# Shared keys and values of the third attention computed during the second feed-forward

## Chip, cores and metric

One core of a Trainium2 chip runs the program. The metric is the device time of one execution in microseconds; of several executions the median is told. 
## What is computed

Eight layers in a row work on x, 32 sequences of 128 tokens with 128 features, with a context of the same shape. Each layer normalises x, computes something, scales it by a gate and adds it to x. The order is attention, feed-forward, four times over:

```python
x = x + tanh(g_xattn[0]) * L0_xattn(layernorm(x), ctx, ctx, ...)   # 16 heads
x = x + tanh(g_ffn[0])   * L0_ffn(layernorm(x), w1, w2)            # quantised
x = x + tanh(g_xattn[1]) * L1_xattn(layernorm(x), ctx, ctx, mask)  # one head
x = x + tanh(g_ffn[1])   * L1_ffn(layernorm(x), gate, up, down)    # quantised, gated
x = x + tanh(g_xattn[2]) * L2_xattn(layernorm(x), ctx, ctx, ...)   # 16 heads, one key and value head
x = x + tanh(g_ffn[2])   * L2_ffn(layernorm(x), switch_w, ...)     # 8 experts
x = x + tanh(g_xattn[3]) * L3_xattn(layernorm(x), ctx, mask, ...)  # 16 heads
x = x + tanh(g_ffn[3])   * L3_ffn(layernorm(x), W_exp, ...)        # butterfly
```

The change concerns L2_xattn. Its 16 query heads share one key head and one value head of 8 features; keys and values depend on the context alone, and the context is an input:

```python
qh = (q @ w_q).reshape(B, L, 16, 8).transpose(0, 2, 1, 3)
kvp = c @ w_kv                      # c is the context, w_kv is 128 x 16
k, v = (kvp[..., :8], kvp[..., 8:])
attn_prob = softmax(einsum('bhid,bjd->bhij', qh, k) / sqrt(8))
out = einsum('bhij,bjd->bhid', attn_prob, v)
```

## The kernel before

The program is written per engine. Each engine has its own list of instructions in a fixed order, and semaphores tie them together. x, the context and its transpose contextT (a column per token) stay in SBUF the whole time, one tile of 128x128 per sequence, 32 tiles.

**Second feed-forward (bit_ffn, called for "F1").** It works on pairs of tiles, 16 of them (NP). A step j touches several pairs at different ages. VectorE takes the largest values of the normalised rows of pair j+4 (L1890), adds the result of pair j to x (L1895), multiplies gate and up part of pair j+2 (L1902), takes their largest values (L1910), works out scales (L1917 to L1929) and rounds pair j+2 (L1942). GpSimd rounds the rows of pair j+4 (L806) and signals bit_qx. TensorE multiplies pair j+3 with the gate and up weights (L1454, L1455), pair j+1 with the down weights (L1467), waits for bit_qx, transposes pair j+4 into bank 6 (L1475) and then the hidden values of pair j+2 (L1485). ScalarE applies silu to pair j+3 (L1043), normalises pair j+5 (L1055), copies the transposed rows (L1062) and the transposed hidden values (L1068) out of PSUM. The first iterations of the third attention are placed between the last steps (TENSOR_BETWEEN, SCALAR_BETWEEN).

**Attention (attention, called for "L0", "L2" and "L3").** Its iteration t does one tile. Each iteration has two halves; a half computes scores for half of the heads of tile t, keys by queries (L1268), and for tile t+2, queries by keys (L1271). VectorE takes row maxima from the latter (L1728), splits them into three bf16 parts, and L1282 subtracts them from the scores as a small matmul; ScalarE takes the exponentials (L944), TensorE multiplies them with the values (L1300). Queries, keys and values are made for four tiles at once, a quad (NQ is 8, QT is 4). In "L2" and "L3" the quad c is transposed at t = 4c - 6 (L1366), the queries are made in the same iteration (L1417), the keys at 4c - 5 with one matmul over 512 columns of contextT (L1373) and the values at 4c - 3 with four matmuls of 128x128 (L1422). All three use one PSUM bank (quad_bank, bank 5) in turn. For "L2" the weights l2_wkv hold the 8 columns of w_kv sixteen times, so keys and values come out once per head. ScalarE copies queries to q_all (L968), keys to k_all (L974) and values into vals (L982), and makes four masked copies of the keys, k_one (L954), on which the queries-by-keys scores run. q_all, k_all, k_one and vals have two halves, for an even and an odd quad.

From t = 7 on the iterations of "L2" also route tiles to the experts: a normed tile is transposed and multiplied with switch_w (L1341, L1405), VectorE picks the expert (hot_experts, L1859 to L1865, after iterations 10, 14, ...), and GpSimd scatters rows to HBM (L856). Where the order of work around the change is set: by the order in which these functions issue, and by semaphores such as t_kn (keys copied), t_ve (values copied), bit_qx (rows rounded).

The context itself (not transposed) is last read by the second attention (L1519). Its memory takes the experts' weights once the scores of the third attention are done (L541, L564).

## Time and profile before

| | us |
|---|---|
| median of 3 runs (1108.57 to 1113.24) | 1110.26 |
| the profiled execution | 1101.8 |
| its span in the profile | 1100.0 |
| TensorE busy, of the span | 918.0 (83%) |
| VectorE busy | 740.9 (67%) |
| ScalarE busy | 684.4 (62%) |
| GpSimd busy | 469.5 (43%) |

In fortieths of the span (27.5 us each) it reads 0.5 to 0.9 from about 250 to 440 us, and 0.9 nearly everywhere else, where 0.9 stands for 90% or more. The stage views further down give these figures for chosen stretches. Busy time says which engine has little room; which engine ends a wait is read from the timeline.

### The profile page before, as it was taken

The numbers are of one execution on the slowest core, as the hardware profiler recorded it, in microseconds if no ns is written. First come the engines' busy times: TensorE is split into PE (matmuls) and PEld (weight loads), VectorE is DVE, ScalarE is ACT, GpSimd is POOL, SyncE is SP. The second block draws the span as 40 slices with busy tenths as digits, with TensorE's granted clock in tenths as the row PEclk, the third lists the DMA queues.
The fourth block names the chain that finished last, engine by engine and source line by source line (L and its number), as shares of the span: only waits on it lengthen the run. The fifth ranks groups of instructions, "written<-read, shape, count | busy, mean of one in ns | idle before, by whom it ended". The sixth has DMA issues, their size and how long they took to land.

```text
span 1100.0 us, 29173 instructions
## 1 busy us (share of the span) xinstructions
PE 918.0 (83%) x9573; PEld 572.6 (52%) x9573; DVE 740.9 (67%) x2005; ACT 684.4 (62%) x1499; POOL 469.5 (43%) x999
## 2 busy tenths in 40 slices
PE   3898889885658665699999988888689899999898
PEld 2744444443436433434545444778664445544698
DVE  2567877756978799868888874246336767666344
ACT  3556666646856566767777643545466677775466
POOL 5422367751134424201143444668541249885200
PEclk9999999995668768899999996989899999999999
DMA  6978778627699993000000002666621001110011
GB/s 177 159 94 93 67 82 90 97 28 183 127 163 167 164 163 41 1 1 2 2 11 11 11 17 60 175 174 181 204 89 49 2 3 41 40 41 2 8 34 36
DMA packets 300443, 84.95 MB, mean 77 GB/s; under 512 B 211929, under 2 KB 287097, under 8 KB 300314
## 3 DMA queue, kind: packets, MB, share of 16 engines
q1 hardware_dynamic: 293962, 67.11, 37.9%
q0 software_dynamic: 5488, 15.88, 4.5%
q8 instruction: 78, 1.28, 0.5%
q10 hardware_dynamic: 864, 0.27, 0.1%
q14 instruction: 51, 0.42, 0.1%
HBM read 50.70 MB, written 35.51 MB: 78 GB/s over the span
## 4 chain that ended last, share of the span: by engine, by line
PE 59%; DVE 22%; issue 9%; POOL 4%; ACT 3%; DMA 2%; SPq 1%; another core or an unknown queue 1%; DVEq 0%; ACTq 0%; POOLq 0%
PE bank L1268 15%; DVE nmax L1728 9%; PE bank L1300 6%; PE bank L1390 3%; PE bank L1580 3%; PE bank L1282 3%; PE bank L1592 3%; PE bank L1634 3%; PE bank L1626 3%; PE bank L1271 2%; DVE small L1910 2%; PE bank L1399 2%; PE bank L1258 2%; PE bank L1417 1%; DVE stats L1663 1%
## 5 line engine op out<-in xcount | busy, mean ns | idle before, releaser
L1728 DVE TENSOR_REDUCE nmax<-bank 128x8 f32<-128x1024 f32 x192 | 234.7, 1223 | 120.7 <-PE bank L1271 119.3
L944 ACT ACTIVATE probs_space<-bank 128x1024 f32<-128x1024 f32 x192 | 196.7, 1024 | 145.4 <-PE bank L1282 144.4
L1268 PE MATMUL bank<-q_one,k_all 32*128 32x512 f32 x768 | 216.7, 633 | 32.5 <-DVE nmax L1728 28.9
L1271 PE MATMUL bank<-k_one,q_all 32*128 32x512 f32 x768 | 214.2, 631 | 2.2 <-DVE nmax L1728 0.9
L1300 PEld LDWEIGHTS bank<-probs_space,vals 128*32 128x32 f32 x3072 | 73.2, 110 | 121.8 <-issue 121.4
L1300 PE MATMUL bank<-probs_space,vals 128*32 128x128 f32 x3072 | 125.6, 282 | 0.0
L1268 PEld LDWEIGHTS bank<-q_one,k_all 32*128 32x128 f32 x768 | 62.1, 185 | 61.6 <-issue 57.8
L954 ACT ACTIVATE k_one<-k_all,one_head 128x512 f32<-128x512 f32 x96 | 68.9, 722 | 20.8 <-DVE k_all L1752 19.3
L640 POOL TENSOR_TENSOR var_b<-stats 128x8 f32<-128x8 f32 (+3 forms) x33 | 7.4, 225 | 170.9 <-DVE stats L1663 168.8
L715 POOL CAST nmax_parts<-nmax 128x16 bf16<-128x16 f32 x64 | 12.7, 198 | 157.6 <-DVE nmax L1728 144.2
L1282 PE MATMUL bank<-nmax_one,ones_bf 12*128 12x512 bf16 x384 | 78.0, 379 | 0.0
L1762 DVE TENSOR_TENSOR nmax_one<-bank,max_row 128x512 bf16<-128x512 bf16 x96 | 65.4, 682 | 2.2 <-PE bank L1347 2.2
L868 POOL DMA_INDIRECT token_rows<-early,slot_row_int x46 | 49.0, 1064 | 41.8 <-DVE early L2098 34.1
L1663 DVE BATCH_NORM_STATS2 stats<-x 128x6 f32<-128x128 f32 x230 | 61.3, 288 | 5.3 <-DMA x<-in_x_dram 2.3
L1580 PE MATMUL bank<-xn,context 128*128 128x128 f32 x368 | 53.5, 292 | 13.4 <-issue 12.0
L2098 DVE TENSOR_TENSOR early<-bank,context 128x128 f32<-128x128 f32 x46 | 13.4, 291 | 72.1 <-PE bank L1592 65.2
L1271 PEld LDWEIGHTS bank<-k_one,q_all 32*128 32x128 f32 x768 | 58.6, 184 | 5.3 <-issue 4.2
L1580 PEld LDWEIGHTS bank<-xn,context 128*128 128x128 f32 x368 | 48.9, 207 | 15.5 <-issue 13.7
L699 POOL TENSOR_TENSOR late<-bf_up,late 128x512 f32<-128x512 f32 x36 | 56.8, 1598 | 0.1
L647 POOL TENSOR_TENSOR var_a<-var_b,minus_half 128x8 f32<-128x8 f32 (+3 forms) x33 | 54.0, 1638 | 2.6
L960 ACT ACTIVATE q_one<-q_all,one_head 128x512 f32<-128x512 f32 x80 | 54.6, 729 | 0.0
L1592 PE MATMUL bank<-moe_w,probs_space 128*128 x368 | 52.4, 288 | 2.3 <-DVE early L2098 1.9
(286 smaller groups left out, 2237.2 us busy)
## 6 DMA issues: line engine op xcount, KB each, us to landing
expert_rows<-zeros SPq DMA_DIRECT2D x8, 2322.0 KB, 37.6
context<-expert_w SPq DMA_DIRECT2D x46, 322.0 KB
late<-_L_ffn_down_weights_dram POOLq DMA_DIRECT2D x9, 512.0 KB, 5.3
late<-in_L_ffn_up_weights_dram POOLq DMA_DIRECT2D x9, 512.0 KB, 4.1
q_one<-expert_rows SPq DMA_DIRECT2D x46, 64.5 KB
q_scratch<-late SPq DMA_DIRECT2D x8, 256.0 KB
v_scratch<-moe_w SPq DMA_DIRECT2D x8, 256.0 KB
vals<-v_scratch SPq DMA_DIRECT2D x8, 256.0 KB
```

The lines of the kernel that those rows point to most:

```text
L699: pool.tensor_tensor(tmp(i), half(src, i % 2), weight, ALU.mult).then_inc(S("bf_step"), 1)
L944: act.activation(probs[:, 2 * g:2 * g + 2, :, :].rearrange("k g i q -> k (g i q)"), bank_pair[1][:, :, :].rearrange("k g f -> k (g f)"), A ...
L954: act.activation(k_one[:, c % 2, i, :], k_all[:, c % 2, :], ACT.Copy, scale=one_head[:, i:i + 1]).then_inc(S("t_k1"), 1)
L1268: pe.matmul(bank[2 + s], group(k_all, u, 2 * g + s), group(q_one, u, 2 * g + s), start=not masked, stop=False)
L1271: m = pe.matmul(bank[s], group(q_all, v, 2 * f + s), group(k_one, v, 2 * f + s), start=not masked, stop=True)
L1282: m = pe.matmul(bank[2 + s], ones_bf[first:last, :], nmax_one[first:last, u % 2, :, :], start=False, stop=True)
L1300: m = pe.matmul(bank[4][32 * j:32 * j + 32, g * P:(g + 1) * P], v[:, first:first + VW], probs[:, 2 * g + j // 2, j % 2 * 2 + s, :], start= ...
L1580: m = pe.matmul(bank[(t + 1) % 2][:, c * P:(c + 1) * P], slot_w1(t + 1)[:, c * P:(c + 1) * P], slot_xT[:, (t + 1) % 2, :], start=True, sto ...
L1592: m = pe.matmul(bank[(4, 6)[(t - 1) % 2]][:, 0:P], slot_hid[:, (t - 1) % 2, c * P:(c + 1) * P], w2[:, bass.ds(expert[t - 1] * HID + c * P, ...
L1663: dve.bn_stats(stats[:, u, :], x[:, u * P:(u + 1) * P]).then_inc(S("stats"), 1)
L1728: dve.tensor_reduce(nmax[:, u % 2, 0, :].rearrange("q (g i) -> q g i", i=HG)[:, 2 * g:2 * g + 2, :], bank_pair[0][:, :, :].rearrange("q g ...
L1762: dve.tensor_tensor(nmax_one[:, (t + 1) % 2, :, :], over_blocks(bank[6][:, 3 * P:4 * P].bitcast(BF16)[:, 0:P], HG), max_row[:, :].unsqueez ...
```

## The change

The keys and values of the third attention are computed in the steps of the second feed-forward. In the step that transposes pair u, TensorE also multiplies l2_wkv with the 256 columns of contextT that belong to the pair (bank 6, columns 256 to 511) and each of the two tiles with 8 columns of the value weights (bank 6, columns 128 to 255, 16 tiles before it is emptied). ScalarE copies the keys into the memory of the untransposed context (shared_keys) and, every eighth pair, the values of 16 tiles into half of k_all (shared_values). The third attention reads its keys from there; its copy into vals repeats the 8 values for all 16 heads. The key and value products and the copy of keys in its iterations are gone; the other two attentions keep theirs. The wait on t_kn and t_ve counts are shifted to match. The iteration at t = -6 waits for all keys and values.

```diff
+        shared_keys = context
...
+        shared_values = k_all[:, 1, 0:NT * DH]
...
+        KEYS_BEFORE = {"L0": 0, "L3": NQ + NP}
...
-                        act.wait_ge(S("t_kn"), quads + c + 1)
-                    act.activation(k_one[:, c % 2, i, :], k_all[:, c % 2, :], ACT.Copy, scale=one_head[:, i:i + 1]
+                        act.wait_ge(S("t_kn"), NQ + 2 * c + 2 if layer == "L2" else KEYS_BEFORE[layer] + c + 1)
+                    keys = shared_keys[:, QT * P * c:QT * P * (c + 1)] if layer == "L2" else k_all[:, c % 2, :]
+                    act.activation(k_one[:, c % 2, i, :], keys, ACT.Copy, scale=one_head[:, i:i + 1]
...
-                    if own and c is not None:
+                    if layer == "L3" and c is not None:
...
                         act.activation(k_all[:, c % 2, :], quad_bank(c), ACT.Copy).then_inc(S("t_kn"), 1)
...
+                    if layer == "L2" and c is not None:
+                        act.wait_ge(S("t_ve"), 2)
+                        past(act, "t_pv", 2 * (tiles + QT * (c - 1)))
+                        act.activation(vals[:, c % 2 * QT:c % 2 * QT + QT, :, 0:DH],
+                                       shared_values[:, QT * DH * c:QT * DH * (c + 1)].rearrange("k (j d) -> k j d", d=DH)
+                                       .unsqueeze(2).broadcast_to([P, QT, NH, DH]), ACT.Copy).then_inc(S("t_ve"), 1)
...
+                        if gated:
+                            act.activation(shared_keys[:, 2 * P * u:2 * P * (u + 1)], bank[6][:, 2 * P:4 * P], ACT.Copy
+                                           ).then_inc(S("t_kn"), 1)
+                            if u % 8 == 7:
+                                act.activation(shared_values[:, u // 8 * P:(u // 8 + 1) * P], bank[6][:, P:2 * P], ACT.Copy
+                                               ).then_inc(S("t_ve"), 1)
...
+                def keys_of(u, g):
+                    return tile_of(shared_keys, u)[HR * g:HR * g + HR, :] if layer == "L2" else group(k_all, u, g)
...
-                    if c is not None and (own or c > 0):
+                    if c is not None and layer != "L2" and (own or c > 0):
...
-                    if own and c is not None:
-                        pe.wait_ge(S("t_kn"), quads + c + 1)
+                    if layer == "L3" and c is not None:
+                        pe.wait_ge(S("t_kn"), KEYS_BEFORE[layer] + c + 1)
...
                         pe.wait_ge(S("bit_qx"), pairs + u + 1)
                         past(pe, "bit_xe", pairs + u)
+                        if gated:
+                            past(pe, "t_kn", NQ + u)
+                            past(pe, "t_ve", u // 8)
+                            pe.matmul(bank[6][:, 2 * P:4 * P], l2_wkv[:, 0, :], contextT[:, 2 * P * u:2 * P * (u + 1)],
+                                      start=True, stop=True)
+                            for n in (2 * u, 2 * u + 1):
+                                at = P + n % 16 * DH
+                                pe.matmul(bank[6][:, at:at + DH], tile_of(contextT, n), l2_wkv[:, 1, 0:DH],
+                                          start=True, stop=True)
                         for r in range(2):
                             m = pe.transpose(xt_bank(layer, u).bitcast(F16)[:, r * P:(r + 1) * P],
...
```

The order of TensorE's instructions in one step of the second feed-forward, before (xqT_bf are the transposed rows, o_heads holds the rounded rows, q_one the hidden values):

```order
L1454 MATMUL bank<-ffn_wT,xqT_bf 128x512 [waits bit_hm,bit_xe]
L1455 MATMUL bank<-ffn_wT,xqT_bf 128x512
L1454 MATMUL bank<-ffn_wT,xqT_bf 128x512 [waits bit_hm]
L1455 MATMUL bank<-ffn_wT,xqT_bf 128x512
L1467 MATMUL bank<-ffn_wT,q_one 128x128 [waits bit_res,bit_he]
L1467 MATMUL bank<-ffn_wT,q_one 128x128 x7
L1475 MATMUL bank<-ident_half,o_heads 128x128 [waits bit_xe,bit_qx]
L1475 MATMUL bank<-ident_half,o_heads 128x128
L1485 MATMUL bank<-ident_half,q_one 128x128 [waits bit_he,bit_hq]
L1485 MATMUL bank<-ident_half,q_one 128x128 x7
```

and after the change, whose line numbers are 25 to 34 higher:

```order
L1479 MATMUL bank<-ffn_wT,xqT_bf 128x512 [waits bit_hm,bit_xe]
L1480 MATMUL bank<-ffn_wT,xqT_bf 128x512
L1479 MATMUL bank<-ffn_wT,xqT_bf 128x512 [waits bit_hm]
L1480 MATMUL bank<-ffn_wT,xqT_bf 128x512
L1492 MATMUL bank<-ffn_wT,q_one 128x128 [waits bit_res,bit_he]
L1492 MATMUL bank<-ffn_wT,q_one 128x128 x7
L1502 MATMUL bank<-contextT,l_wkv 128x256 [waits t_kn,t_ve,bit_xe,bit_qx]
L1506 MATMUL bank<-l_wkv,contextT 128x8 x2
L1509 MATMUL bank<-ident_half,o_heads 128x128 x2
L1519 MATMUL bank<-ident_half,q_one 128x128 [waits bit_he,bit_hq]
L1519 MATMUL bank<-ident_half,q_one 128x128 x7
```

The key product L1502 and the two value products L1506 stand between the down product and the transposes of the rounded rows, and the wait for bit_qx is now in front of them.

ScalarE in one step after the change, one in which values are copied too:

```order
L1053 ACTIVATE q_one<-bank,small 128x512 [waits bit_hm,bit_hp] x2
L1065 ACTIVATE xn_quad<-x,shift,rstd 128x128 [waits norms,bit_qx]
L1065 ACTIVATE xn_quad<-x,shift,rstd 128x128
L1072 ACTIVATE xqT_bf<-bank 128x256 [waits bit_hp,bit_xt]
L1075 ACTIVATE context<-bank 128x256
L1078 ACTIVATE k_all<-bank 128x128
L1084 ACTIVATE q_one<-bank 128x1024 [waits bit_yp,bit_ht]
```

Before, L1072 (there L1062) is followed directly by L1084 (L1068); L1075 and L1078 are new.

TensorE in the third attention around the value products of quad 2, at t = 5, before:

```order
L1300 MATMUL bank<-probs_space,vals 32x128 [waits t_ve,t_ue,t_ex]
L1300 MATMUL bank<-probs_space,vals 32x128 x7
L1390 MATMUL bank<-l_wo,oT 128x128 [waits t_res,t_oe,t_on,t_nm]
L1399 MATMUL bank<-ident,o_heads 128x128 [waits t_ue]
L1399 MATMUL bank<-ident,o_heads 128x128
L1422 MATMUL bank<-l_wkv,contextT 128x128 [waits t_kn]
L1422 MATMUL bank<-l_wkv,contextT 128x128 x3
L1268 MATMUL bank<-q_one,k_all 128x512 [waits t_qa,t_k1,t_ex,t_mx,t_q01,t_q23]
L1271 MATMUL bank<-k_one,q_all 128x512
```

and after, in the same place:

```order
L1319 MATMUL bank<-probs_space,vals 32x128 [waits t_ve,t_ue,t_ex]
L1319 MATMUL bank<-probs_space,vals 32x128 x7
L1415 MATMUL bank<-l_wo,oT 128x128 [waits t_res,t_oe,t_on,t_nm]
L1424 MATMUL bank<-ident,o_heads 128x128 [waits t_ue]
L1424 MATMUL bank<-ident,o_heads 128x128
L1287 MATMUL bank<-q_one,context 128x512 [waits t_qa,t_k1,t_ex,t_mx,t_q01,t_q23]
L1290 MATMUL bank<-k_one,q_all 128x512
```

The four value products are gone, and the scores read their keys from context.

## Rows read from the trace of the kernel before

**Rows 1.** Stages: stretch, its us, PE, PEld, DVE, ACT, POOL busy, clock, DMA, GB/s
```profile
378.00:465.00 87.00, 54.43 (x358) 30.32 (x359) 78.11 (x219) 57.91 (x101) 28.28 (x62) 0.73 0.62 78
536.00:636.00 100.00, 94.49 (x1060) 50.96 (x1063) 81.64 (x237) 70.15 (x132) 40.64 (x105) 1.00 0.04 12
```

**Rows 2.** TensorE's waits, 395 to 455 us: total us, times, longest us
```profile
PE bank L1475 <- POOL o_heads L806: 18.1, 12, 2.3
```

**Rows 3.** Timeline of the second feed-forward: start us, us, engine, line, operation
```profile
431.92 0.23 DVE L1929 TENSOR_SCALAR small<-small,ffn_sw 128x2 f32<-128x2 f32 x1
...
432.24 1.20 POOL L806 TENSOR_SCALAR o_heads<-xn_quad,small 128x128 f32<-128x128 f32 x2 [3.73 <-DVE small L1929]
...
433.50 0.29 PE L1475 MATMUL bank<-ident_half,o_heads 128*128 128x128 f16 x2 [1.12 <-POOL o_heads L806]
...
433.82 0.38 ACT L1062 ACTIVATE xqT_bf<-bank 128x256 bf16<-128x256 f16 x1 [0.81 <-PE bank L1475]
...
434.27 1.02 ACT L1068 ACTIVATE q_one<-bank 128x1024 bf16<-128x1024 f16 x1
...
435.41 1.27 ACT L1043 ACTIVATE q_one<-bank,small 128x512 f32<-128x512 f32 x2
...
436.58 0.87 ACT L1055 ACTIVATE xn_quad<-x,shift,rstd 128x128 f32<-128x128 f32 x2
...
437.98 0.41 DVE L1890 TENSOR_REDUCE small<-xn_quad 128x2 f32<-128x256 f32 x1
...
441.98 0.22 DVE L1929 TENSOR_SCALAR small<-small,ffn_sw 128x2 f32<-128x2 f32 x1
```

**Rows 4.** Groups, 490 to 650 us: count, busy us, mean ns, idle before
```profile
L1373 PE MATMUL bank<-contextT,l_wkv 128*128 128x512 f32 x12 | 6.5, 620 | 0.0
...
L1422 PE MATMUL bank<-l_wkv,contextT 128*128 128x128 f32 x51 | 7.2, 283 | 0.0
...
L1405 PE MATMUL bank<-switch_w,xnT 128*128 128x8 f32 x42 | 6.0, 216 | 0.0
...
L994 ACT ACTIVATE o_heads<-bank 128x256 f32<-128x256 f32 x26 | 9.9, 380 | 0.0
...
L974 ACT ACTIVATE k_all<-bank 128x512 f32<-128x512 f32 x6 | 3.5, 591 | 0.0
```

**Rows 5.** Timeline of the third attention, quads 2 and 3, TensorE
```profile
510.89 0.42 PE L1282 MATMUL bank<-nmax_one,ones_bf 12*128 12x512 bf16 x2
...
512.36 1.06 PE L1422 MATMUL bank<-l_wkv,contextT 128*128 128x128 f32 x8
...
514.31 0.39 PE L1282 MATMUL bank<-nmax_one,ones_bf 12*128 12x512 bf16 x2
...
520.28 0.39 PE L1282 MATMUL bank<-nmax_one,ones_bf 12*128 12x512 bf16 x2
...
521.50 1.08 PE L1373 MATMUL bank<-contextT,l_wkv 128*128 128x512 f32 x2
...
523.47 0.39 PE L1282 MATMUL bank<-nmax_one,ones_bf 12*128 12x512 bf16 x2
...
526.09 0.39 PE L1282 MATMUL bank<-nmax_one,ones_bf 12*128 12x512 bf16 x2
```

**Rows 6.** Timeline of the third attention, last quads
```profile
635.62 0.96 POOL L856 DMA_INDIRECT expert_rows<-late,dest_int  x1 [0.30 <-issue]
...
636.58 0.26 DVE L1789 RECIPROCAL o_inv<-bank 128x16 f32<-128x16 f32 x1 [1.59 <-remote]
...
637.39 0.60 ACT L982 ACTIVATE vals<-bank 128x512 f32<-128x512 f32 x1 [2.82 <-remote]
...
642.76 0.39 PE L1282 MATMUL bank<-nmax_one,ones_bf 12*128 12x512 bf16 x2
...
646.85 0.42 PE L1282 MATMUL bank<-nmax_one,ones_bf 12*128 12x512 bf16 x2
```

**Rows 7.** Timeline, the first query product at the lower clock
```profile
459.86 2.02 PE L1417 MATMUL bank<-xnT_quad,l_wq 128*128 128x512 f32 x2 [1.07 <-ACT xnT_quad L1009]
```

More of the change, by code:

```diff
@@ L970, in iteration @@
                     c = quad(t, 4)
-                    if own and c is not None:
+                    if layer == "L3" and c is not None:
                         past(act, "t_s2", 2 * (tiles + QT * (c - 1)))
-                        act.wait_ge(S("t_kp"), quads + c + 1)
+                        act.wait_ge(S("t_kp"), NQ + c + 1)
                         act.activation(k_all[:, c % 2, :], quad_bank(c), ACT.Copy).then_inc(S("t_kn"), 1)
@@ L978, in iteration @@
                     c = quad(t, 2)
-                    if own and c is not None:
-                        act.wait_ge(S("t_vp"), own_quads + c + 1)
+                    if layer == "L3" and c is not None:
+                        act.wait_ge(S("t_vp"), c + 1)
                         past(act, "t_pv", 2 * (tiles + QT * (c - 1)))
@@ L1267, in pair_of_scores @@
                         if live(u):
-                            pe.matmul(bank[2 + s], group(k_all, u, 2 * g + s), group(q_one, u, 2 * g + s),
+                            pe.matmul(bank[2 + s], keys_of(u, 2 * g + s), group(q_one, u, 2 * g + s),
                                       start=not masked, stop=False)
@@ L1292, in weighted_values @@
                         if own:
-                            pe.wait_ge(S("t_ve"), own_quads + u // QT + 1)
+                            pe.wait_ge(S("t_ve"), 2 + own_quads + u // QT + 1)
                         else:
@@ L1311, in iteration @@
                         pe.wait_ge(S("bit_ge"), 2 * 2 * NP)
+                        pe.wait_ge(S("t_ve"), 2)
+                        pe.wait_ge(S("t_kn"), NQ + NP)
                     if layer == "L2" and t == -3:
@@ L1360, in iteration @@
                             pe.wait_ge(S("t_xn"), own_tiles + QT * (c + 1))
-                            past(pe, "t_ve", own_quads + c)
                         else:
                             pe.wait_ge(S(f"L0_q{c % 2}"), 16 * (c // 2 + 1))
-                        past(pe, "t_kn", quads + c)
+                        if layer == "L2":
+                            past(pe, "t_qa", quads + c)
+                        else:
+                            past(pe, "t_kn", KEYS_BEFORE[layer] + c)
+                        if layer == "L3":
+                            past(pe, "t_ve", 2 + own_quads + c)
                         for j in range(QT):
@@ L1418, in iteration @@
                     c = quad(t, 3)
-                    if own and c is not None:
-                        pe.wait_ge(S("t_kn"), quads + c + 1)
+                    if layer == "L3" and c is not None:
+                        pe.wait_ge(S("t_kn"), KEYS_BEFORE[layer] + c + 1)
                         for j in range(QT):
@@ L1424, in iteration @@
                         m.then_inc(S("t_vp"), 1)
-                        if layer == "L2" and c == 0:
-                            fill_wait(8, 3)
+                    if layer == "L2" and c == 0:
+                        fill_wait(8, 3)
                     if not own:
@@ L1534, in _ @@
                 last_iteration = attention("L3")
-                pe.wait_ge(S("t_ve"), NQ)
+                pe.wait_ge(S("t_ve"), NQ + 2)
                 w2 = moe_w2[:, :, :, :].rearrange("f e c d -> f (e c d)")
```

## Prediction, written before the changed kernel had run

> **What bounds the kernel now.** I read the stage windows first, because the change takes work out of one stage and puts it into another. From 378 to 465 us, the second feed-forward, VectorE is busy for 78 of 87 us and TensorE for 54, at a mean granted clock of 0.73. From 536 to 636 us, inside the third attention, TensorE is busy for 94 of 100 us at full clock and VectorE for 82 [rows 1]. So work seems to leave TensorE where it is full and to go where it has room. The share of busy time does not say which wait ends last, so each stage was read again.
>
> The second feed-forward handles a pair of tiles per step. The waits show where TensorE's room lies: 18.1 us in 12 steps, in front of the transposes of the rounded rows (L1475), for GpSimd's rounding (L806) [rows 2]. That wait is a link of a ring. VectorE's scales (L1929) end at 432.15; GpSimd rounds to 433.44; TensorE transposes; ScalarE runs L1062, L1068, the two silus and the norm of a later pair (L1055), which ends at 437.45; VectorE takes that at 437.98 (L1890) and its scales end at 442.20 [rows 3]. The ring spans two steps: 5.30 us up to L1055's end and 4.22 us from L1890 on, 9.52 us, with 0.53 us of slack. From L1929 at 431.92 to L1929 at 441.98 is 10.06 us, 5.03 a step. VectorE has no gap there worth the name; but the ring comes within half a microsecond of being the bound.
>
> In the third attention the distance between two score groups (L1282) is a half iteration. A plain one takes 2.62 us (523.47 to 526.09). The half that holds the four value products (L1422, 1.06 us) takes 3.42, the half with the key product (L1373, 1.08 us) 3.19 [rows 5]. What remains of a plain half is the ring from scores to VectorE's maxima and back. That holds for the first quads. From the routing on VectorE has more to do: at 642.76 to 646.85, in the last quad, where no key product is left, the same half still takes 4.09 us [rows 6]. And at four of the value halves VectorE starts late (L1789, 1.59 us of idle time, right as GpSimd's scatter L856 ends), and ScalarE 0.8 us behind it [rows 6].
>
> **What is taken out of the third attention.** Eight key products, 32 value products and eight copies of keys leave; the eight copies into vals read SBUF in place of PSUM. TensorE's work falls by about 2.1 us per quad, 17 us in all, but only what a half loses counts.
> - Values of quads 1 to 3: 3.42 - 2.62 = 0.80 us each, three of them: 2.4 us.
> - Keys of quads 2 and 3: 3.19 - 2.62 = 0.57 us each: 1.1 us. Quads 0 and 1 have theirs in the head.
> - Keys of quads 4 to 7: VectorE's expert choice delays the next maxima, as the 4.09 us without a key product show. I take nothing.
> - Values of quads 4 to 7: the late start of VectorE stays, and it ends with the scatter [rows 6], which is not touched. For quads 4 and 5 the exponentials come last, behind the copy into vals; that copy now needs no product, and I take 0.5 us each, 1.0 us. For 6 and 7 nothing.
> - Head: the copy of k_all (0.59 us, [rows 4]) stands between L1068 and the four k_one copies that the first scores wait for: 0.6 us. The value products there end long before those copies and are worth nothing, since fill matmuls follow.
>
> Together 5.1 us. The copy into vals gets dearer (the same size from SBUF, k_one's, is a tenth of a microsecond dearer); in a half of 2.62 us beside an exponential of 1.02 it fits. If every key and value half gained fully, it would be 7 x 0.57 + 7 x 0.80 + 0.6 = 10.2 us; if the middle ones gave nothing, 4.1 us.
>
> **What is put into the second feed-forward.** Each of the 16 steps issues one key product over 256 columns and two value products over 8 columns, on TensorE after the wait for L806 and ahead of L1475: not in the 18.1 us of waiting but behind it, on the ring. ScalarE gets a copy of 128x256 between L1062 and L1068, and twice one of 128x128.
> - Key product: half of L1373's 1.08 us, 0.54 us [rows 4, 5].
> - Value products: the nearest row is L1405, also 128x8 with full weights, 6.0 us busy for 21 products, 0.29 us each [rows 4]. Two are 0.58 us apart and less in a row; I take 0.4, and 0.1 for the weights' arrival after the wait. Sum 1.05 us.
> - Copy: L994's 0.38 us [rows 4], of which 0.07 fills the gap that stands there today and some overlaps: 0.25 us.
>
> The ring becomes 9.52 + 1.05 + 0.25 = 10.82 us, 5.41 a step: 0.38 above 5.03, and now it bounds in place of VectorE. That is at full clock. At the lower level one product over 512 columns takes 2.02 us (L1417, [rows 7]), so the additions are 2.0 us there, on a ring that then is already the bound at 10.06: (10.06 + 2.0)/2 = 6.03 a step, 1.0 more. The stage's clock is 0.73 [rows 1], but more work in it means fewer and shorter gaps, so I take a value nearer the full clock, 0.5 us. The ring closes 14 times: 7.0 us. In the start-up of the stage, at the lower clock, the first additions stand on the path once more: 1 us. Together 8 us; bounds: 14 x 0.38 = 5.3 us and 14 x 1.0 + 2 = 16 us; below nothing if the clock rises so that TensorE's part of the ring shortens by more than the additions: 14 x 0.1 = 1.4 us of gain, down to VectorE's own 4.93.
>
> Nothing moves on SyncE, GpSimd or VectorE, and no DMA is added. The wait that the head gains (keys and values all computed) is met long before. The context is free after the second attention, and the expert weights that later go there wait for the third attention's scores, as now.
>
> **The sum.** -5.1 + 8 = +3 us on the profiled execution's 1101.8 us. That execution lies 8.5 us below the median of the three runs (1110.26), so for a median I say **1113.3 us**. About 0.5%, 5.5 us, is what a measurement can tell from no change.
>
> **The clock, by trace and page.** The trace shows both levels within one step: in this stage the clock falls after the long waits and comes back while TensorE works. The Trainium skill (TensorE: Matmul & The Clock Gate, What's actually happening) says that throttling is the default and that activity releases it. By that rule the added products would bring the stage to 2.4 GHz altogether; the step would then be the 5.41 above, and the sum 5.3 + 0.5 - 5.1 = +0.7 us.
>
> **Rivals.**
> 1. *The products run at the lower clock* (slower). Place: TensorE behind the wait for L806, each step. For it: the wait for L806 is the longest gap of the step, and it stays; the clock is 0.73 now. Against: TensorE's work per step rises by a third. Price up to 1.0 us per step: +16 - 5 = +11 us, 1121. It decides from a step of about 5.7 us on, where the stage alone costs 14 x 0.7 + 1 = 11 us and the sum passes +5.5.
> 2. *The ring has more give than I read, and TensorE's relief counts fully* (faster). If the key product overlaps the wait's tail and L1890 absorbs 0.5 us per ring, the stage costs 2 us, and if the late halves also gain, 10 us leave: -8 us, 1102. For it: TensorE's 94%. Against: the 4.09 us half and the order of the queue, in which the wait comes first.
> 3. *The copy into vals delays the exponentials* (within it, or just slower). It reads 8 values for 16 heads each. If it took twice k_one's time, 1.4 us, it would hold the value halves near their 3.42 us: -1.7 + 8 = +6 us. Against: ScalarE is idle for more than a quarter of the stage [rows 1].
> 4. *The change doesn't cut what it says*: the four value products and the key product are gone from the order below, so I give it nothing.
>
> **Chances.** Forecast, step between 5.3 and 5.65 us, sum between -2 and +5.5: 0.47. Rival 1: 0.27. Rival 3: 0.06. Rival 2: 0.20. Faster by over 0.5%: 0.20. Slower by over 0.5%: rivals 1 and 3, 0.33. Within: 0.47. Range: below, it goes most of the way to rival 2, -6 us; above, to the low-clock bound of 1121 and the value of rival 3 with it: 1104 to 1122. The forecast's own range is 1108 to 1116.
>
> **What would show it.** Right: distance of two L1929 (its line after the change) 10.8 us or more, with L1890 idle and ScalarE's L1055 as its releaser; VectorE's busy share in the stage falls from 0.90 to about 0.82; plain halves of 2.6 us at the first value and key halves of the attention, but late quads within half a microsecond of their old length; the first L1282 of the attention comes about 7 us later than before and its last about 3 us later. Wrong: a step of 5.0 us (then the additions hide and the sum is -5 or better), a step near 6 us (rival 1), or late quads shorter by over 1 us.

## The result and the profile after

| | before | changed | ratio, 95% interval |
|---|---|---|---|
| median, us | 1109.37 (16 runs) | 1116.89 (16 runs) | 1.0064 [1.0049, 1.0079] |
| profiled execution, us | 1101.8 | 1117.02 | |
| its span, us | 1100.0 | 1115.3 | |

Slower by 7.1 us [5.4, 8.7]: inside the stated range of 1104 to 1122, 0.9 us past the forecast's own 1108 to 1116, and just past the 0.5% that I had set as the bound of no change.

Where the 15.3 us between the two spans lie is read from the starts of four instructions: the first bit_inv scales (L1929 before, L1963 after), the first and the last score group with the negated maxima (L1282, L1301), and GpSimd's last return of expert rows (L868, L871).

| stretch, us | before | changed | difference |
|---|---|---|---|
| start to first bit_inv | 377.1 | 380.1 | +3.0 |
| first bit_inv to first score group ("feed-forward" below) | 103.0 | 111.3 | +8.2 |
| first to last score group ("attention" below) | 192.8 | 196.6 | +3.8 |
| last score group to last return ("experts" below) | 146.0 | 148.3 | +2.2 |
| rest | 281.0 | 279.1 | -1.9 |

The profiled execution of before lies 7.6 us below its median, so not all 15 us are the change's. The first row is no work of the change: over 14 traces it lies between 377.1 and 381.2 for all kernels.

The stage windows of the changed kernel, two stretches that answer to [rows 1] (columns as there):

```profile
381.00:475.00 94.00, 65.49 (x433) 45.41 (x442) 77.47 (x216) 58.71 (x117) 27.98 (x62) 0.77 0.54 72
549.00:655.00 106.00, 90.13 (x1024) 47.33 (x1017) 82.95 (x239) 68.85 (x128) 43.68 (x112) 0.96 0.04 12
```

VectorE's share in the feed-forward fell from 0.90 to 0.82, TensorE's in the attention from 0.94 to 0.85, and there the clock is 0.96 where it was 1.00. The waits from 390 to 465 us, which answer to [rows 2]:

```profile
PE bank L1502 <- POOL o_heads L809: 18.5, 12, 2.2
DVE small L1924 <- ACT xn_quad L1065: 7.3, 8, 1.9
```

TensorE still waits as long for GpSimd's rounding, now in front of the key product L1502. New is VectorE's wait for ScalarE's norm, eight times and 7.3 us (in the same window before: once, 0.4 us): the ring bounds. One turn of it in the timeline, answering to [rows 3]:

```profile
434.68 0.22 DVE L1963 TENSOR_SCALAR small<-small,ffn_sw 128x2 f32<-128x2 f32 x1
...
434.99 1.19 POOL L809 TENSOR_SCALAR o_heads<-xn_quad,small 128x128 f32<-128x128 f32 x2 [3.73 <-DVE small L1963]
...
436.62 1.17 PE L1502 MATMUL bank<-contextT,l_wkv 128*128 128x256 f32 x2
437.49 0.42 DVE L1924 TENSOR_REDUCE small<-xn_quad 128x2 f32<-128x256 f32 x1 [1.81 <-ACT xn_quad L1065]
437.58 0.76 PE L1506 MATMUL bank<-l_wkv,contextT 128*128 128x8 f32 x4
...
438.19 0.27 PE L1509 MATMUL bank<-ident_half,o_heads 128*128 128x128 f16 x2
...
438.50 0.39 ACT L1072 ACTIVATE xqT_bf<-bank 128x256 bf16<-128x256 f16 x1 [1.04 <-PE bank L1509]
438.78 0.38 ACT L1075 ACTIVATE context<-bank 128x256 f32<-128x256 f32 x1
439.05 1.03 ACT L1084 ACTIVATE q_one<-bank 128x1024 bf16<-128x1024 f16 x1
...
443.07 0.70 PE L1502 MATMUL bank<-contextT,l_wkv 128*128 128x256 f32 x2 [2.22 <-POOL o_heads L809]
...
443.97 0.27 PE L1509 MATMUL bank<-ident_half,o_heads 128*128 128x128 f16 x2
```

From L1502's start to the transposes behind it (L1509) it takes 1.57 us here and 0.90 us a step later. Over the 16 steps there are ten of 0.85 to 1.05 us and six of 1.57 to 1.73: full and lower clock, 1.20 us in the mean. On ScalarE the distance from L1072 to L1084 is 0.55 us in such a step at full clock, where it was 0.45 [rows 3]. The distances of two L1963 run unevenly from 4.61 to 6.93 us; in the mean of the 13 behind the start-up they are 5.50 us, where L1929 had 5.02. The start-up distance ahead of them is 10.5 us, it was 8.7.

In the attention, the early half iterations ("halves" below; the value half is the one that held the value products, the key half the one with the key product) did what was said: behind L1301 at 507.84, where a key product used to be, one takes 2.59 us (before 3.08 to 3.19), and the value halves take 2.61 to 2.65 in all quads (before 3.15 to 3.64):

```profile
504.49 0.40 PE L1301 MATMUL bank<-nmax_one,ones_bf 12*128 12x512 bf16 x2
507.84 0.39 PE L1301 MATMUL bank<-nmax_one,ones_bf 12*128 12x512 bf16 x2
510.43 0.42 PE L1301 MATMUL bank<-nmax_one,ones_bf 12*128 12x512 bf16 x2
```

The late quads did not. The half behind the value half took 3.38 to 3.44 us before; in quads 4 to 7 it now takes 4.38, 5.65, 5.24 and 6.16. Quad 5, answering to [rows 6]:

```profile
591.06 0.42 PE L1301 MATMUL bank<-nmax_one,ones_bf 12*128 12x512 bf16 x2
...
592.31 0.38 PE L1424 MATMUL bank<-ident,o_heads 128*128 128x128 f32 x2
592.44 0.62 ACT L991 ACTIVATE vals<-k_all 128x512 f32<-128x512 f32 x1
...
593.61 0.96 POOL L859 DMA_INDIRECT expert_rows<-late,dest_int  x1 [0.30 <-issue]
593.71 0.39 PE L1301 MATMUL bank<-nmax_one,ones_bf 12*128 12x512 bf16 x2
...
595.42 0.26 DVE L1823 RECIPROCAL o_inv<-bank 128x16 f32<-128x16 f32 x1 [2.45 <-remote]
595.59 1.02 ACT L947 ACTIVATE probs_space<-bank 128x1024 f32<-128x1024 f32 x1 [2.53 <-PE bank L1301]
...
596.54 0.33 PE L1357 MATMUL bank<-ident,o_tok 128*128 128x128 f32 x1 [1.87 <-DVE late L1854]
...
599.36 0.71 PE L1301 MATMUL bank<-nmax_one,ones_bf 12*128 12x512 bf16 x2
```

By the records VectorE's input (from L1424) is there at 592.7 and the scores for ScalarE at 594.1, yet the two begin only at 595.4 and 595.6, 0.8 us and more behind the end of the last scattered write (594.57). "Remote" means that the view found no releaser on this core's engines. After that TensorE waits, and the matmuls at 599.36 take 0.71 us, the lower clock. This was the open question for the experiments.

### The profile page after: what moved, and what is told of

It reads as the page before. It is cut to its first block, busy times and chain, and to the rows that moved or that the text cites. A ratio compares the mean times of both kernels' runs of the same rounds, so it can differ in the third digit from the quotient of the medians.

```text
span 1115.3 us, 29202 instructions
## 1 busy us (share of the span) xinstructions
PE 928.2 (83%) x9576; PEld 585.0 (52%) x9589; DVE 740.5 (66%) x2005; ACT 682.0 (61%) x1509; POOL 468.0 (42%) x999
## 4 chain that ended last, share of the span: by engine, by line
PE 56%; DVE 23%; issue 10%; POOL 5%; ACT 3%; DMA 2%; another core or an unknown queue 1%; SPq 1%; DVEq 0%; ACTq 0%; POOLq 0%
PE bank L1287 14%; DVE nmax L1762 10%; PE bank L1319 6%; PE bank L1415 3%; PE bank L1614 3%; PE bank L1626 3%; PE bank L1668 3%; PE bank L1660 3%; PE bank L1301 2%; PE bank L1290 2%; PE bank L1424 2%; PE bank L1277 2%; DVE small L1944 2%; DVE stats L1697 1%; PE bank L1195 1%
## 5 line engine op out<-in xcount | busy, mean ns | idle before, releaser
L1290 PE MATMUL bank<-k_one,q_all 32*128 32x512 f32 x768 | 218.4, 643 | 3.4 <-DVE nmax L1762 1.7
L1287 PE MATMUL bank<-q_one,k_all 32*128 32x512 f32 x512 | 144.6, 634 | 19.4 <-DVE nmax L1762 16.4
L1287 PE MATMUL bank<-q_one,context 32*128 32x512 f32 x256 | 77.4, 675 | 15.2 <-DVE nmax L1762 14.9
L718 POOL CAST nmax_parts<-nmax 128x16 bf16<-128x16 f32 x64 | 12.6, 196 | 161.9 <-DVE nmax L1762 146.0
L1301 PE MATMUL bank<-nmax_one,ones_bf 12*128 12x512 bf16 x384 | 79.5, 386 | 0.0
L871 POOL DMA_INDIRECT token_rows<-early,slot_row_int x46 | 48.8, 1060 | 44.2 <-DVE early L2132 35.8
L1287 PEld LDWEIGHTS bank<-q_one,k_all 32*128 32x128 f32 x512 | 41.6, 186 | 32.0 <-issue 31.4
L958 ACT ACTIVATE k_one<-k_all,one_head 128x512 f32<-128x512 f32 x64 | 45.9, 721 | 20.1 <-DVE k_all L1786 19.3
L1823 DVE RECIPROCAL o_inv<-bank 128x16 f32<-128x16 f32 x96 | 24.5, 255 | 47.5 <-PE bank L1424 37.7
```

The lines of the kernel that those rows point to most:

```text
L1287: pe.matmul(bank[2 + s], keys_of(u, 2 * g + s), group(q_one, u, 2 * g + s), start=not masked, stop=False)
L1290: m = pe.matmul(bank[s], group(q_all, v, 2 * f + s), group(k_one, v, 2 * f + s), start=not masked, stop=True)
L1301: m = pe.matmul(bank[2 + s], ones_bf[first:last, :], nmax_one[first:last, u % 2, :, :], start=False, stop=True)
```

## The experiments

They ran on three chips, four kernels on each. There the kernel before takes 1082.45, 1080.31 and 1080.63 us, 2.5% less than in the pair above. The number of the first pair's chip is not known; from this difference it is called the 1st and taken for a fourth, but one of the three in another condition isn't excluded. Each kernel's whole is compared with the kernel before on its own chip. Lengths of stretches are those of the table above, each from one profiled execution.

| run | chip | feed-forward | attention | experts | against before, us [95%] |
|---|---|---|---|---|---|
| before, first pair | 1st | 103.0 | 192.8 | 146.0 | |
| changed, first pair | 1st | 111.3 | 196.6 | 148.3 | +7.1 [5.4, 8.7] |
| f1_alone | 2nd | 111.0 | 185.3 | 128.5 | +5.3 [2.7, 7.9] |
| l2_alone | 2nd | 103.2 | 178.5 | 128.8 | -8.4 [-11.8, -5.1] |
| ahead | 2nd | 101.1 | 178.6 | 128.7 | -11.5 [-15.5, -7.5] |
| keys_only | 2nd | 105.8 | 184.1 | 131.7 | +4.0 [1.6, 6.3] |
| before_again | 3rd | 102.3 | 186.8 | 131.7 | +0.9 [-1.8, 3.6] |
| after_again | 3rd | 110.3 | 177.1 | 128.5 | +1.3 [-1.7, 4.2] |
| ahead_pe | 3rd | 101.0 | 177.3 | 128.9 | -6.9 [-10.3, -3.6] |
| after_noscatter | 3rd | 110.6 | 179.0 | 128.2 | one execution, 1078.88 us |
| ahead_again | 4th | 101.2 | 177.2 | 132.7 | -9.1 [-12.5, -5.7] |
| act_late | 4th | 111.8 | 177.2 | 132.4 | +1.3 [-1.5, 4.1] |
| ahead_fill | 4th | 104.1 | 178.7 | 127.9 | -9.7 [-13.1, -6.4] |
| ahead_fill2 | 4th | 108.9 | 181.3 | 129.8 | -3.5 [-6.8, -0.2] |

**The feed-forward's part alone.** From the kernel before, with the new products and copies added under signals of their own:

```diff
                         past(pe, "bit_xe", pairs + u)
+                        if gated:
+                            past(pe, "x_kn", u)
+                            past(pe, "x_ve", u // 8)
+                            pe.matmul(bank[6][:, 2 * P:4 * P], l2_wkv[:, 0, :], contextT[:, 2 * P * u:2 * P * (u + 1)],
+                                      start=True, stop=True)
...
```

> The kernel before with the new products and ScalarE copies in the second feed-forward alone; the third attention still computes and uses its own keys and values, so the new ones are written and never read. Theory A (the feed-forward's ring carries the cost, and the attention's loss seen in the two traces belongs to the attention's own edits): the time from the first bit_inv of the feed-forward to the first score matmul with the negated maxima grows from 103.0 us by 7 to 9, the attention from there to its last such matmul stays at 192.8 (within 1), and the whole is +7 to +9 us. Rival B (the attention suffers from what it inherits from the feed-forward, its later start against GpSimd's work or the clock): the feed-forward grows the same, but the attention grows by 3 or more as well, +10 to +13 us in all.

The feed-forward grew by 8 us, as expected; the whole, +5.3, reaches the +7 only with its interval. The attention fits neither theory: 185.3 us, 7.5 less than before on the first chip, in a kernel whose attention's work is that of before.

**The attention's part alone.** From the changed kernel, without the additions:

```diff
-                        act.wait_ge(S("t_kn"), NQ + 2 * c + 2 if layer == "L2" else KEYS_BEFORE[layer] + c + 1)
+                        if layer != "L2":
+                            act.wait_ge(S("t_kn"), KEYS_BEFORE[layer] + c + 1)
...
-                        if gated:
-                            past(pe, "t_kn", NQ + u)
...
```

> The changed kernel without the new products and copies in the second feed-forward; its attention reads stale data in the keys' and values' places, so its results differ and the routing of the tokens with them, but it issues the same instructions. Theory A (taking the value products out of an iteration lays bare a stall near GpSimd's four scattered writes): the quads 4 to 7 have a value half of 2.6 us followed by one of 4.4 to 6.2 us, the attention is 193 to 197 us long, and the whole is 0 to +4 us. Rival B (the attention's edits are a gain as predicted, and what was lost came in with the feed-forward): the attention is 187 to 189 us long and the whole is -4 to -6 us.

Theory A falls: the attention is 178.5 us long, 6.8 less than f1_alone's on the same chip, and the whole gains 8.4 us. Rival B has the sign but neither the size (it said 187 to 189 us and -4 to -6) nor the reason, since f1_alone's attention did not suffer from its feed-forward either.

**Keys alone.** The value products and their copy from PSUM go back into the attention:

```diff
-                    if layer == "L3" and c is not None:
+                    if own and c is not None:
...
-                            for n in (2 * u, 2 * u + 1):
...
```

> The changed kernel with the keys alone moved to the feed-forward; the attention computes its value products in their old half iteration and ScalarE copies them from PSUM as before. Theory A (the value products covered the stall): the value half of the quads 4 to 7 is 3.6 us again and the half behind it 3.4 to 3.5, the attention is 191 to 193 us long, 3 to 5 us shorter than in the changed kernel; the feed-forward is 4 to 7 us longer than before (value products of 0.42 us a step gone), and the whole is +3 to +5. Rival B (the stall depends on the place of the attention against GpSimd's work, not on the value products): the halves behind the value halves are 4.4 us or more in three of the quads 4 to 7 all the same, and the attention is 195 us or more.

The halves behind the value halves are 2.6 to 2.7 us in all quads, with value products (3.64) as without (2.65 in l2_alone). So it is not the value products that cover a stall; on this chip there is none. The lengths expected by Theory A were missed with it: the attention takes 184.1 us (191 to 193 expected), and the feed-forward is 2.5 us longer than l2_alone's and 2.8 to 3.5 longer than that of the kernel before in its two traces, where I had 4 to 7. Without the two value products, which with the gap to the transposes are some 0.4 us a step, the stage costs less than half of its 8 us.

**Both kernels on one chip.** To settle that, both kernels, unedited:

> The kernel before, for a profile from the chip of the other runs of this call. Theory D (the stall beside GpSimd's scattered writes belongs to the chip of the first pair and not to a kernel): on a chip like that of the first four experiments, where the kernel before takes some 1082 us, the third attention is 184 to 186 us long and the half behind the value half is 2.7 us in the quads 4 to 7; on a chip like the first, where it takes some 1110 us, 192 to 194 us and 3.4 us. The ratio is 1 within 0.002 in either case.

> The changed kernel on the same chip. Theory D (the parts add, and the stall comes from the chip): where the chip shows no stall, the feed-forward is 8 us longer than before and the attention 6.5 to 7.5 us shorter, as the two parts were alone, so the whole is -3 to +3 us (from f1_alone's +5.5 and l2_alone's -8.3, a sum of -2.8); where it shows the stall, the attention is 3 to 4 us longer and the whole is +6 to +9, as in the first pair. Rival E (together the parts cost what neither costs alone): the attention of the changed kernel has halves of 4 us and more behind its value halves, and the whole is +5 us or more, on a chip on which the kernel before has none over 3.7 there.

Theory D holds as to the stall: in the quads 4 to 7 the halves behind the value halves take 2.59 to 2.73 us in the kernel before and 2.69 to 2.73 in the changed one. Its lengths were missed, 186.8 us where it had 184 to 186, and 9.7 us shorter where it had 6.5 to 7.5. The kernel before shows on the third chip, in quad 5, a half behind the value half of 2.72 us (589.07 to 591.79), ScalarE waiting 1.30 us for the value products:

```profile
587.25 0.25 DVE L1789 RECIPROCAL o_inv<-bank 128x16 f32<-128x16 f32 x1
587.98 0.96 POOL L856 DMA_INDIRECT expert_rows<-late,dest_int  x1 [0.30 <-issue]
588.21 0.60 ACT L982 ACTIVATE vals<-bank 128x512 f32<-128x512 f32 x1 [1.30 <-PE bank L1422]
589.07 0.39 PE L1282 MATMUL bank<-nmax_one,ones_bf 12*128 12x512 bf16 x2
...
591.79 0.39 PE L1282 MATMUL bank<-nmax_one,ones_bf 12*128 12x512 bf16 x2
```

On the first chip the same instructions of the same kernel, same quad:

```profile
585.85 0.96 POOL L856 DMA_INDIRECT expert_rows<-late,dest_int  x1 [0.30 <-issue]
586.19 0.26 DVE L1789 RECIPROCAL o_inv<-bank 128x16 f32<-128x16 f32 x1 [0.99 <-PE bank L1399]
586.94 0.39 PE L1282 MATMUL bank<-nmax_one,ones_bf 12*128 12x512 bf16 x2
587.68 0.60 ACT L982 ACTIVATE vals<-bank 128x512 f32<-128x512 f32 x1 [2.90 <-remote]
```

And in the changed kernel on the third chip the reciprocal beside the scatter has no wait, where on the first it had 2.45 us:

```profile
586.89 0.62 ACT L991 ACTIVATE vals<-k_all 128x512 f32<-128x512 f32 x1
587.34 0.25 DVE L1823 RECIPROCAL o_inv<-bank 128x16 f32<-128x16 f32 x1
588.06 0.95 POOL L859 DMA_INDIRECT expert_rows<-late,dest_int  x1 [0.30 <-issue]
588.16 0.39 PE L1301 MATMUL bank<-nmax_one,ones_bf 12*128 12x512 bf16 x2
```

There the two parts work against each other: feed-forward +8.1, attention -9.7, whole +1.3 [-1.7, 4.2], no change that can be measured. (The two profiled executions alone differ by -8.6 us, since that of the changed kernel lies 6 us below its median; traces give the stages, medians the whole.)

Not all of the -9.7 is the change's. From the first score group to the end of the value half of quad 7, the old attention takes 154.6 us in before_again and in f1_alone, the new one 146.4 to 146.8 in the nine traces on these chips: 8.2 us of gain. The third and fourth half behind that value half, of which the third is the one that took 4.09 us in [rows 6], hold 1.7 us of the difference: together they take 8.3 and 6.7 us in before_again and f1_alone, whose attention does the same work, and 6.6 to 8.6 in the nine others. The sum of the parts alone on the second chip, -3.1, has an interval of about 4 us and does not contradict it.

> The changed kernel without GpSimd's scattered writes to the experts' rows (their signals are given by GpSimd itself, the rows stay zero, and the rows returned to the tokens start as zeros by one more write before the third attention), for the lengths of the attention's halves alone. If the chip shows the stall in after_again: with the writes as its cause, the halves behind the value halves of quads 4 to 7 fall from 4.4 to 6.2 us to 2.7; with another cause they stay. If it shows none, this kernel's attention is within 1.5 us of after_again's, and the run says only that the writes cost nothing on such a chip.

In place of the four writes per quad stands one signal each:

```diff
-                        pool.indirect_dma_start(
...
+                        pool.sem_inc(S(f"scattered_{c % 4}"), 16)
```

The chip had no stall, so the question could not be put: 179.0 us against 177.1, a little more than the 1.5 us I had allowed and not less; 1.7 of the 1.9 us lie in the two halves just named.

**The products ahead of the wait.** The order on TensorE is turned round, and ScalarE's copies go behind L1084:

```diff
-                        pe.wait_ge(S("bit_qx"), pairs + u + 1)
-                        past(pe, "bit_xe", pairs + u)
                         if gated:
                             past(pe, "t_kn", NQ + u)
...
+                        pe.wait_ge(S("bit_qx"), pairs + u + 1)
+                        past(pe, "bit_xe", pairs + u)
```

> The changed kernel with the key and value products put ahead of TensorE's wait for GpSimd's rounded quad, and ScalarE's copies of them put behind its copy of the transposed hidden values. Theory A (the new work costs time because it stands inside the ring of the feed-forward behind the rounding): TensorE's 1.05 us falls into its wait of 1.5 us a step and leaves the ring, so the feed-forward is 2 to 6 us longer than before instead of 8.2, and the whole is 3 to 6 us below the changed kernel. Rival C (the new work costs because DVE, ScalarE and TensorE together have no slack, wherever it stands): the feed-forward stays 7 to 9 us longer than before and the whole stays at +7.

Better than Theory A: the feed-forward is 2.1 us shorter than l2_alone's, which has none of the products, and the whole is 11.5 us below before. Its timeline:

```profile
433.41 0.95 PE L1501 MATMUL bank<-contextT,l_wkv 128*128 128x256 f32 x2
433.49 1.19 POOL L809 TENSOR_SCALAR o_heads<-xn_quad,small 128x128 f32<-128x128 f32 x2 [3.74 <-DVE small L1964]
434.20 0.51 PE L1505 MATMUL bank<-l_wkv,contextT 128*128 128x8 f32 x4
434.29 0.42 DVE L1925 TENSOR_REDUCE small<-xn_quad 128x2 f32<-128x256 f32 x1
...
434.74 0.29 PE L1510 MATMUL bank<-ident_half,o_heads 128*128 128x128 f16 x2
```

The products run while GpSimd rounds, the transposes follow 0.06 us behind the rounding, and VectorE's reduce has no wait. TensorE's wait from 395 to 450 us shrinks to this:

```profile
PE bank L1510 <- POOL o_heads L809: 9.8, 7, 1.6
```

**Which of the two moves counts.** Products ahead, copies left; the same kernel as ahead once more; and copies late, products left:

> The changed kernel with the products alone put ahead of TensorE's wait for the rounded quad; ScalarE's copies stay between its copy of the transposed quad and that of the hidden values. Theory A (TensorE's part of the ring was the cost, and ScalarE's copies have slack): like ahead, a feed-forward 2 us shorter to 1 us longer than before and the whole within 3 us of ahead's -11 to -14. Rival F (ScalarE's copy of 0.6 us before the hidden values' copy is in the ring too): the feed-forward is 3 to 6 us longer than before, and the whole 4 us or more above ahead's.

> The kernel of the run ahead once more, to stand beside the three others on one chip. Theory A: -9 to -13 us against the kernel before on a chip without the stall, the feed-forward 0 to 2.5 us shorter than before. Were its first result an accident of the runs, it would be within 5 us of before. On a chip with the stall (the kernel before at some 1110 us): the feed-forward as well 0 to 2.5 us shorter, the attention 2 to 4 us longer than before, the whole -1 to +3 us.

> The changed kernel with ScalarE's copies of keys and values put behind its copy of the hidden values, and TensorE's products left behind the wait for the rounded quad. Theory A (the ring is lengthened by TensorE's products, 1.05 us, and hardly by ScalarE's 0.38 us): the feed-forward is 6 to 8.5 us longer than before, at most 2 us less than the changed kernel's +8. Rival F (ScalarE's copies carry a good part): the feed-forward is 2 to 5 us longer than before.

ahead_pe's feed-forward and experts are ahead's to 0.2 us, and its attention is 1.3 us shorter, by the two halves named above; its whole, -6.9, misses my bound of 3 us from ahead, but the two intervals overlap and no stage is longer by more than 0.2 us. ahead_again confirms the gain. act_late has no gain: its 111.8 us are 8.6 to 9.5 above the stage without products (102.3 to 103.2 in three traces), a little more than I had expected at most. So the cost was TensorE's place in the ring, and none is seen on ScalarE.

**Work put back into the ring.** ahead with the key product computed once or twice more behind the wait:

```diff
                         past(pe, "bit_xe", pairs + u)
+                        if gated:
+                            for _ in range(2):
+                                pe.matmul(bank[6][:, 2 * P:4 * P], l2_wkv[:, 0, :],
+                                          contextT[:, 2 * P * u:2 * P * (u + 1)], start=True, stop=True)
```

> ahead with the key product computed once more (into the same place) behind the wait for the rounded quad: about 0.5 us of TensorE work a step put back into the ring, none on ScalarE. Theory A (the ring of 9.52 us for two steps lies 0.1 to 0.2 us a step under what VectorE takes by itself, and from there each 0.5 us in it lengthens a step by 0.25, or by more where TensorE's clock is at its lower level): the feed-forward is 1 to 4 us longer than ahead's. Rival G (TensorE's place in the order does not matter, ahead gained because the copies moved): the feed-forward is within 1 us of ahead's.

> The same with two such products behind the wait, about 1.0 us a step, as much as the changed kernel has there. Theory A: the feed-forward is 5 to 9 us longer than ahead's, near the changed kernel's, and more than twice what the first one cost, since the first used up the slack. Rival H (a cost in proportion, with no slack before it): twice that of ahead_fill within 1 us. Rival G: within 1 us of ahead's.

+2.9 us and +7.8 us of feed-forward over ahead_again: the first inside 1 to 4, the second inside 5 to 9 and more than twice the first, as Theory A has it; from Rival H's 5.8 it is 2.0 away, past its 1 us. VectorE's wait for the norm is back in ahead_fill2, from 395 to 450 us:

```profile
DVE small L1929 <- ACT xn_quad L1065: 4.8, 5, 2.7
```

The whole of ahead_fill (-9.7) does not show its 2.9 us against ahead_again's -9.1; the intervals are wider than that, and its experts stretch happened to be 4.7 us shorter. That stretch takes 127.9 to 132.7 us in the twelve traces on these chips, without relation to the edits.

## Why the prediction was right, and where not

**The total was in the range partly by luck.** The sum said +3 us and the medians give 7.1 [5.4, 8.7], past the forecast's upper end of +5.5. I had slower by over 0.5% at 0.33, by rivals 1 and 3 alone; it came true without either at its price. The upper end of 1122 was set by rival 1, and what filled the room was an attention that didn't gain. On the third chip the whole, +1.3 [-1.7, 4.2], agrees with +3, there with an attention that gained more than I had.

**The feed-forward's +8 was right, and so was its reason.** Measured 8.2 and 8.1 us in two pairs (8 predicted). The reduce waits for the norm; f1_alone shows it without any change in the attention, ahead takes the products off the ring and the cost is gone, ahead_fill2 puts as much back and it returns. The terms were off in ways that cancelled: TensorE's additions are 0.90 us at full clock where I had 1.05, ScalarE's 0.10 where I had 0.25, but six of 16 steps ran the products at the lower clock, 1.6 to 1.7 us. The step came to 5.50 us, the 5.53 that I took (5.03 + 0.5), so the 13 steps cost 6.2 us (I had 14 x 0.5 = 7.0) and the start-up 1.8 (I had 1.0). Rival 1 was right on the mechanism in six steps out of 16, and its 5.7 us a step wasn't reached.

**The attention's -5.1 was wrong on the first chip, and on the others as well, the other way.** There it was 3.8 us longer in the profiled pair, on the third chip 9.7 shorter, 8.2 of it by the change. By the steps of the prediction:
- Values of quads 1 to 3, 2.4 us: 2.3 us in both pairs. Keys of quads 2 and 3, 1.1 us: 1.1. Right.
- Keys of quads 4 to 7, nothing: 1.1 us in all on the third chip (3.23, 3.19, 3.35, 3.33 to 3.08, 3.03, 2.96, 2.96). Small, but not nothing. The half of 4.09 us from which I took the nothing is not like these: it takes 3.15 to 4.70 us over the fourteen traces, with no key product in it, where the key halves took 3.2 to 3.4.
- The last quad behind its value half, in which I counted nothing: nothing that can be put down to the change. The third chip's pair shows 1.7 us there, in the two halves that take 6.6 to 8.6 us on these chips whatever the kernel.
- Head, 0.6 us, which lies in the feed-forward's stretch: not seen. l2_alone, with the attention's edits alone, takes 103.2 us there, the kernel before 103.0 and 102.3.
- **Values of quads 4 to 7: "the late start of VectorE stays, and it ends with the scatter". This step failed.** The late start in [rows 6] isn't a property of the kernel: the twelve later traces lack it, those of the same two kernels included. Without it each of these halves gave its whole 1.0 us, 4.0 in place of my 1.0. With it, the halves lost 1.0 us each and the ones behind them grew by 0.9 to 2.8 us. I had supposed the end of the stall fixed by the scatter, and that the copy into vals was the only thing behind it; in fact the next half held the rest, with TensorE idle and once at the lower clock. ScalarE's wait of 2.82 us in [rows 6] is 1.30 us on the third chip, and its releaser is the product.

The medians on the first chip, +7.1 with +8.2 from the feed-forward, leave room for an attention near -1 in most executions, so that the profiled pair would overstate its loss; no second trace there shows it.

**Rivals 2 and 3.** Rival 2 was half right on chips without the stall: TensorE's relief counts for 8.2 us of the 9.6 that my 10.2 has without the head, but the ring had no give. Rival 3 has nothing for it: the value halves with the copy from SBUF (0.62 us, L991, beside my bound of 1.4) take 2.65 us.

**The signs.** "Right" by my list: the share 0.90 to 0.82, the plain halves, the first score group 7 us later (11.2, of which 3.0 stood before the stage). A step of 5.4 us: 5.50. Wrong: the last score group, 15.0 us later in place of about 3. "Late quads within half a microsecond of their old length" does not hold: on the first chip the eight halves around quad 5 are 2.1 us longer, and on the third chip value and key half of each late quad are together over 1 us shorter, which stood among my signs of being wrong.

**The clock.** The rows from 380 to 450 us of before, after, before_again, after_again and ahead_fill2, in this order (the clock is the third number from the end):

```profile
380.00:450.00 70.00, 42.95 (x285) 23.88 (x285) 64.81 (x179) 47.30 (x83) 22.00 (x46) 0.72 0.74 92
```
```profile
380.00:450.00 70.00, 47.95 (x306) 33.55 (x313) 56.35 (x159) 41.66 (x83) 21.51 (x49) 0.74 0.74 98
```
```profile
380.00:450.00 70.00, 38.66 (x264) 21.24 (x270) 63.02 (x176) 45.19 (x79) 23.86 (x51) 0.74 0.79 101
```
```profile
380.00:450.00 70.00, 46.56 (x326) 31.84 (x330) 58.23 (x161) 45.20 (x90) 20.49 (x44) 0.84 0.70 92
```
```profile
380.00:450.00 70.00, 53.54 (x378) 38.07 (x384) 57.90 (x161) 44.50 (x89) 21.39 (x47) 0.94 0.58 81
```

On the third and fourth chip TensorE is busy for 39, 47 and 54 of 70 us at a clock of 0.74, 0.84 and 0.94. The first pair, with 43 and 48 us, stays at 0.72 and 0.74. Nor does busy time order the others: 42.8 us go with 0.67 in l2_alone and 0.80 in keys_only, 50.9 us with 0.81 in ahead and 51.4 with 0.93 in ahead_fill; and a matmul at the lower clock is itself busy for longer. That activity releases the throttle, as the Trainium skill has it (TensorE: Matmul & The Clock Gate, What's actually happening), is borne out by some of these rows only. The stage did not come to full speed with the change, as I had followed the rule to.

**Open.** What the first chip does beside GpSimd's scattered writes, and whether it is the chip or a condition that it was in: nothing ran on it again. From 480 to 690 us its two traces have 16.3 and 12.8 us of VectorE's and ScalarE's waits for "remote", the twelve others none. It differs from the others only where GpSimd issues indirect writes: its attention is 6 us longer in the kernel before (4.7 of them in the last three halves, behind the last scattered writes) and its experts stretch 14.3 us (146.0 and 131.7), while the feed-forward (103.0 and 102.3) and the rest (281.0 and 280.7) agree. That the writes are the cause is argued, not shown; the run without them met a chip without the stall. Whether ahead gains on such a chip wasn't tried either.

## What to carry to other kernels

A wait on one engine is room only for work placed in front of it: the same products cost 8 us behind TensorE's wait for the rounding and less than nothing ahead of it, so when work is moved into another stage's idle time, it goes ahead of the wait and the ring of waits is written out before its place is chosen. And a stall whose releaser the trace calls "remote" may belong to the chip or its condition and not to the kernel: before a term rests on it, look at the same kernel on another chip. Here the version with the products ahead is 7 to 12 us faster than the kernel before on three chips, and 8 us faster than the changed one on the chip where both ran (ahead_pe and after_again).

## What the runs showed of the hardware

The same program differs from one place to another by more than the change was worth: it took 1109.4 us in the first pair and 1080.3 to 1082.5 on three chips, and between the traces the difference lies in the two stretches with GpSimd's indirect writes. In the first pair, beside such a write, VectorE's reciprocal started 2.7 us behind the recorded end of the matmuls that it reads, and ScalarE's exponential 1.5 us.

More TensorE work went with a faster stage: with the products ahead, the feed-forward is 2.1 us shorter than the same stage without any (101.1 against 103.2 on one chip; 101.0 against 102.3 on another), at a granted clock of 0.81 from 380 to 450 us against 0.67 (0.84 against 0.74). That the clock is the cause is argued and not shown.
